# A three-pass attention: the mask carried in 32 contraction rows, the second pass one and a half quads behind, the maxima's parts made on GpSimd

## The chip, the core and the metric

One core of a Trainium2 chip runs the whole program. The metric is device time in microseconds (us). Six layers follow each other in one launch; barriers stand between the stages, so a stage that ends later moves everything behind it.

## The reference, cut to what matters

The layer that is changed is an attention over sets of keys. 4 sequences of 1024 tokens, 16 heads of size 16. The keys are sums over aligned blocks of 4, 8, 16, ... tokens, and a token sees a set only when it lies wholly before or at it; a tail of 1 to 4 tokens is added:

```python
K = _get_slice(k_cum, l_idx, r_idx)          # 511 sets
V = _get_slice(v_cum, l_idx, r_idx)
mask = t[:, None] >= r_idx[None, :]
att_logits = jnp.einsum('bhtd,bhsd->bhts', q, K) * scale
att_logits = jnp.where(mask[None, None], att_logits, -jnp.inf)
att_tail = jnp.sum(q * K_tail, axis=-1) * scale
logits = jnp.concatenate([att_logits, att_tail[..., None]], axis=-1)
att = jax.nn.softmax(logits, axis=-1)
out = jnp.einsum('bhts,bhsd->bhtd', att[..., :-1], V) + att[..., -1:] * V_tail
```

Before it stands a quantised linear layer with a LoRA (`first_ffn`), behind it another one, then a mixture of experts, a linear attention and a second mixture of experts. They are not touched.

## The kernel before

**`first_ffn`** (line 165 on) also makes constants on GpSimd: the identity, a mask `mask_f` of 128 x 256 by 16 affine_select instructions (lines 189 to 201), and flags. VectorE casts the mask to `mask_ts`; TensorE turns it for `mask_st`.

**`attention_front`** (line 507) makes, for each of the 4 sequences, the transposed input, the sums over sets (`larger` on VectorE), the tails (four GpSimd instructions, lines 601 to 604), the projections on TensorE, and three bf16 parts of the queries and keys (`split` on VectorE). The parts go to DRAM. TensorE works in order through a ring of 8 PSUM banks; the product of the sets with the value weights needs the banks that VectorE frees in `products`, which stands behind `sets` and `split` in VectorE's queue.

**`attention_main`** (line 795) works on quads: 4 heads of one sequence, so NQ = 16 quads. `q_hat` and `k_hat` hold one quad: 6 combinations of parts give 96 contraction rows (MROW), rings of 5 buffers. SyncE loads a quad by 12 DMAs of 64 or 128 KB.

- Pass A (`scores_a`) computes tokens by sets, 24 pieces per quad (4 heads, 6 groups of tiles of 128 tokens). Each tile first gets a 128-column matmul with the identity that writes the mask, and then the product is added. VectorE takes the maximum over the sets (`highest`). Three PSUM banks serve pass A, two serve pass B while both run (5 where one runs alone).
- `maxima` on VectorE (step M) joins the tail's logit and splits the negated maxima in three bf16 parts. Step MT turns the parts on TensorE, ScalarE copies them out, and SyncE writes them by 3 DMAs as contraction rows 96 to 98 of `q_hat`; the same rows of `k_hat` hold ones, from a memset at the start.
- Pass B (`scores_b`) computes sets by tokens with 99 rows, 24 pieces per quad: 6 blocks (t = 0 to 5; 512, 256, 512, 512, 512, 256 columns) for 4 heads each. In blocks 0, 1, 4 and 5 a 256-column mask matmul goes first. ScalarE takes the exponential into `prob`.
- `values` multiplies `prob` with the values, two blocks at a time, right after the third block behind has been issued: three bursts per quad.
- O1, O2, O3 (for 8 tiles of each finished sequence, at every 8th step) turn the result, turn the normalised one and project it, all through PSUM bank 7, which MT uses too. VectorE's part of them is `normal` and `update`, GpSimd's is the tail's values (line 938).

The order is one list, STEPS, that every engine walks through. In it, one step of quad i's pass A alternates with one of quad i - 2's pass B:

```python
for i in range(NQ + 2):
    a = [("A", i, h, t) ...] if i < NQ else []
    b = [("B", i - 2, h, t) ...] if i >= 2 else []
```

MT of quad i - 1 stands ahead of step 6. So 48 steps of A run alone, 336 steps run both, 48 steps of B run alone. M stands behind all steps of its quad. SyncE loads quads 1 to 3, the output weights and the router's, and then writes the first maxima.

Of the kernel before, what the change touches and what calls it, by code (L numbers as in the profile page):

```python
# [17 lines left out]
ALU = mybir.AluOpType  # L18
# [112 lines left out]
def first_ffn(nc, s, o, w_dram, b_dram, a_dram, lora_b_dram, x_dram):  # L131
# [35 lines left out]
    with nc.Block(no_gpsimd_drain=True) as block:  # L167
# [13 lines left out]
        def _(pool):  # L181
# [7 lines left out]
            for level in range(7):  # L189
                n, size, at = 64 >> level, 4 << level, P - (P >> level)  # L190
                for half in range(2):

                    v = mask_f[:, half * P + at:half * P + at + n]
                    chain.link(nc.gpsimd.affine_select(out=v, in_=v, compare_op=ALU.is_ge, fill=MASKED,
                                                       base=half * P - size + 1, pattern=[[-size, n]],
                                                       channel_multiplier=1))
            for half in range(2):
                v = mask_f[:, half * P + P - 1:half * P + P]
                nc.gpsimd.affine_select(out=v, in_=v, compare_op=ALU.is_ge, fill=MASKED, base=half * P - 2 * P + 1,
                                        pattern=[[0, 1]], channel_multiplier=1).then_inc(mask_made, 1)  # L200
                pool.wait_ge(mask_made, half + 1)
# [3 lines left out]
            chain.link(nc.gpsimd.affine_select(out=o.row_keep[:, 0:1], in_=o.row_keep[:, 0:1], compare_op=ALU.is_ge,  # L205
                                               fill=0.0, base=P - 2, pattern=[[0, 1]], channel_multiplier=-1))
# [43 lines left out]
        def _(v):  # L250
# [54 lines left out]
            v.wait_ge(mask_made, 2)  # L305
            nc.vector.tensor_copy(o.mask_ts[:].rearrange("p h t -> p (h t)"), mask_f[:])
# [23 lines left out]
        def _(pe):  # L330
# [27 lines left out]
            pe.wait_ge(mask_made, 2)  # L358
# [63 lines left out]
SC = SETS // P  # L422
MASKED = -1e30
# [48 lines left out]
def alloc_attention(nc):  # L472
# [5 lines left out]
    o.mask_ts = sb("mask_ts", [P, 2, P], BF16)  # L478
# [5 lines left out]
    o.k_parts = nc.dram_tensor("k_parts", (BATCH, NPART, C, SETS), BF16, kind="Internal").ap()  # L484
    o.v_tails = nc.dram_tensor("v_tails", (BATCH, P, BT, C), F32, kind="Internal").ap()
# [20 lines left out]

def attention_front(nc, s, o, wqkv_dram):
# [14 lines left out]
    v_tail = sb("v_tail", [P, BT, C])  # L522

# [35 lines left out]
    with nc.Block(no_gpsimd_drain=True) as block:  # L559
        @block.sync  # L560
        def _(sp):
            banks.start(sp)
            sp.dma_start(w[:], wqkv_dram.rearrange("(k p) f -> p k f", p=P)).then_inc(w_in, 16)
            for b in range(BATCH):
# [12 lines left out]
                for n in range(NPART):  # L577
                    sp.wait_ge(k_split, NPART * b + n + 1)
                    sp.dma_start(o.k_parts[b, n].rearrange("(k p) t -> p k t", p=P), k_part[:, z, n]).then_inc(k_out[z], 16)
            for z in range(2):  # L580
                sp.wait_ge(q_out[z], 16 * NPART * BATCH // 2)
                sp.wait_ge(k_out[z], 16 * NPART * BATCH // 2)
            sp.wait_ge(vt_out, 16 * BATCH)
            sp.wait_ge(first_in, 16 * (len(K_PARTS) + len(Q_PARTS)))

        @block.gpsimd
        def _(pool):
            chain = Chain(pool, pool_chain)
            for b in range(BATCH):
# [14 lines left out]
                nc.gpsimd.tensor_tensor(t4[:, :, 3], t4[:, :, 2], x4[:, :, 3], ALU.add).then_inc(tails_made, 1)  # L604

        @block.vector
        def _(v):
# [10 lines left out]
            def larger(of):  # L618

                flat = of.rearrange("p c j i -> p (c j) i")  # L620
                for level in range(1, 7):
                    lo, at, n = P - (2 * P >> level), P - (P >> level), 64 >> level
                    chain.link(nc.vector.tensor_tensor(flat[:, :, at:at + n], flat[:, :, lo:at:2],
                                                       flat[:, :, lo + 1:at:2], ALU.add))
                pairs = of.rearrange("p c (h j) i -> p (c h) j i", j=2)
                nc.vector.tensor_copy(pairs[:, :, 0, P - 1:P], pairs[:, :, 0, P - 2:P - 1])
# [2465 lines left out]
```

## Time and profile before

| | us |
|---|---|
| median of 3 runs | 1725.73 |
| lowest, highest | 1715.12, 1725.94 |
| the profiled execution, its own time | 1731.76 |
| its span from first to last instruction | 1730.0 |
| `attention_front`, last TensorE work to next stage | about 62 to 200 |
| `attention_main` | about 200 to 592 |

| engine | busy us of the span |
|---|---|
| PE (matmul) | 1430.8 (83%) |
| PEld (weight load) | 1072.4 (62%) |
| DVE (VectorE) | 987.9 (57%) |
| ACT (ScalarE) | 690.3 (40%) |
| POOL (GpSimd) | 561.3 (32%) |

The shares are means over stages with different limits; a stage is read from its own stretch. A matmul's duration in the trace holds its latency. What TensorE can do per time shows in the distance between the starts of matmuls that follow each other, called pitch below.

### The profile page before, as it was taken

To read this page: it belongs to the slowest core of one execution; us is meant where nothing else is said; L and a number is where in the kernel's file an instruction comes from. 1 tells how busy PE (TensorE), PEld (TensorE's weight loads), DVE (VectorE), ACT (ScalarE), POOL (GpSimd) and SP (SyncE) were. 2 spreads that over 40 slices of the span, in tenths; PEclk is the share of its full clock that TensorE was granted. 3 is DMA by queue.
4 is the path that set the end of the run, shared out by engine and by line. 5 is a ranking of instruction groups with operands and counts; after the bars stand their busy time and mean duration, and the time that the engine had idled before them with its cause. 6 is when DMAs were issued, how large, how long until landed. Compare 5 with 4: busy or idle time off the path is not lost. (4 is left out here: it accounts for less than half of the span.)

```text
span 1730.0 us, 26233 instructions
## 1 busy us (share of the span) xinstructions
PE 1430.8 (83%) x9328; PEld 1072.4 (62%) x9328; DVE 987.9 (57%) x2872; ACT 690.3 (40%) x1640; POOL 561.3 (32%) x465
## 2 busy tenths in 40 slices
PE   6899889999999678447999999289895459999993
PEld 5566544555555456227889889166663348888893
DVE  8887777787874488884541111256676855521120
ACT  4222147666666377434422222003333425323221
POOL 6522300000000344304436654322211232637644
PEclk9989989999999889658999999599997569999997
DMA  3034563324210023315769996501112325879983
GB/s 108 19 130 136 126 124 61 81 56 83 46 38 2 1 85 110 149 22 137 233 195 276 237 286 132 138 19 49 37 49 100 120 64 187 270 211 257 263 224 41
DMA packets 113483, 211.95 MB, mean 123 GB/s; under 512 B 20069, under 2 KB 79370, under 8 KB 104138
## 3 DMA queue, kind: packets, MB, share of 16 engines
q1 hardware_dynamic: 87338, 178.93, 32.5%
q0 software_dynamic: 26016, 31.34, 11.6%
q8 instruction: 76, 1.25, 0.3%
q14 instruction: 53, 0.43, 0.1%
HBM read 158.71 MB, written 51.12 MB: 121 GB/s over the span
## 5 line engine op out<-in xcount | busy, mean ns | idle before, releaser
L952 DVE TENSOR_REDUCE attnm_top<-psum 128x1 f32<-128x384 f32 (+3 forms) x384 | 212.7, 596 | 60.6 <-PE psum L1037 56.5
L1174 ACT ACTIVATE attnm_prob<-psum 128x512 f32<-128x512 f32 (+1 forms) x384 | 192.1, 530 | 90.2 <-PE psum L1047 83.6
L2553 DVE SCALAR_TENSOR_TENSOR moe1e_h<-moe1e_gate,psum 128x160 f32<-128x160 f32 x160 | 50.1, 320 | 195.2 <-ACT moe1e_gate L2491 167.5
L2553 DVE SCALAR_TENSOR_TENSOR moe2e_h<-moe2e_gate,psum 128x160 f32<-128x160 f32 x160 | 50.2, 320 | 191.9 <-ACT moe2e_gate L2491 162.2
L2356 POOL DMA_INDIRECT out<-moe2e_y,moe_scatter_i x74 | 116.2, 1570 | 117.7 <-DMA out<-moe2e_y,moe_scatter_i 64.0
L2356 POOL DMA_INDIRECT x_sum<-moe1e_y,moe_scatter_i x74 | 116.1, 1569 | 115.6 <-DMA x_sum<-moe1e_y,moe_scatter_i 68.0
L2425 PE MATMUL psum<-moe2e_xgT,moe_w_up 128*128 128x160 f32 x1024 | 150.0, 304 | 1.0 <-issue 1.0
L2425 PE MATMUL psum<-moe1e_xgT,moe_w_up 128*128 128x160 f32 x1024 | 149.6, 303 | 0.9 <-issue 0.9
L2425 PEld LDWEIGHTS psum<-moe2e_xgT,moe_w_up 128*128 128x128 f32 x1024 | 144.5, 193 | 4.2 <-issue 3.2
L2425 PEld LDWEIGHTS psum<-moe1e_xgT,moe_w_up 128*128 128x128 f32 x1024 | 144.3, 193 | 4.0 <-issue 3.0
L1348 POOL DMA_INDIRECT moe_xg<-xn_rows,moe_gather_i x80 | 84.2, 1053 | 156.8 <-DVE moe_gather_i L1537 92.9
L938 POOL TENSOR_TENSOR attnm_tail_v<-attnm_v_tail,attnm_tail_p 128x256 f32<-128x256 f32 x32 | 19.9, 622 | 345.6 <-PE psum L1089 284.7
L1035 PE MATMUL psum<-attn_mask_ts,ident_bf 128*128 128x128 bf16 x512 | 105.4, 226 | 11.8 <-DVE attnm_top L952 7.9
L1037 PE MATMUL psum<-attnm_k_hat,attnm_q_hat 96*128 96x512 bf16 (+3 forms) x384 | 106.3, 305 | 0.0
L1047 PE MATMUL psum<-attnm_q_hat,attnm_k_hat 99*128 99x512 bf16 (+1 forms) x288 | 98.4, 345 | 1.1 <-ACT attnm_prob L1174 0.3
L2491 ACT ACTIVATE moe2e_gate<-psum 128x160 f32<-128x160 f32 x160 | 47.1, 301 | 107.3 <-PE psum L2425 87.7
L2491 ACT ACTIVATE moe1e_gate<-psum 128x160 f32<-128x160 f32 x160 | 47.2, 302 | 104.0 <-PE psum L2425 88.2
L1035 PEld LDWEIGHTS psum<-attn_mask_ts,ident_bf 128*128 128x128 bf16 x512 | 50.5, 100 | 50.0 <-issue 24.5
L1060 PE MATMUL psum<-attnm_prob,attn_v_aug 128*32 128x512 f32 (+1 forms) x768 | 78.7, 527 | 0.0
L1045 PE MATMUL psum<-attn_mask_st,ident_bf 128*128 128x256 bf16 x256 | 70.2, 276 | 5.2 <-DMA attn_q_first<-attnm_mT 5.1
L87 DVE BATCH_NORM_STATS2 x_stats<-x_res 128x6 f32<-128x256 f32 x128 | 44.5, 411 | 36.8 <-DMA x_res<-x_sum 36.2
L2439 PE MATMUL psum<-moe_w_down,moe2e_h 128*128 128x256 f32 x256 | 61.2, 382 | 2.0 <-DMA moe_w_down<-in_expert_down 2.0
(420 smaller groups left out, 3111.3 us busy)
## 6 DMA issues: line engine op xcount, KB each, us to landing
moe_w_up<-in_expert_up SPq DMA_DIRECT2D x64, 1024.0 KB
moe_w_down<-in_expert_down SPq DMA_DIRECT2D x64, 512.0 KB
attnm_q_hat<-q_parts SPq DMA_DIRECT2D x72, 128.0 KB, 4.7
moe_a_up<-in_adapter_up SPq DMA_DIRECT2D x32, 256.0 KB
q_parts<-attnf_q_part SPq DMA_DIRECT2D x12, 512.0 KB, 2.8
attnm_k_hat<-k_parts SPq DMA_DIRECT2D x72, 64.0 KB, 2.3
x_res<-in_x SPq DMA_DIRECT2D x8, 512.0 KB
v_tails<-attnf_v_tail SPq DMA_DIRECT2D x4, 1024.0 KB, 5.3
```

The costliest lines, as they stand in the source:

```text
L952: nc.vector.tensor_reduce(top[:, n // QUADS % 2, tiles[0]:tiles[-1] + 1, hh:hh + 1], s.ps[:, u.bank, 0:len(tiles) * width].rearrange("p (t ...
L1035: nc.tensor.matmul(out[:, width - P:width], s.identb[:], o.mask_ts[:, tile % 2, :], start=(i == 0), stop=False, skip_group_check=True)
L1037: ins = nc.tensor.matmul(out, q_hat[r][0:MROW, h, tile * P:(tile + 1) * P], k_hat[r][0:MROW, h, 0:width], start=False, stop=True, skip_gro ...
L1045: nc.tensor.matmul(s.ps[:, u.bank, at:at + 2 * P], s.identb[:], o.mask_st[:], start=True, stop=False, skip_group_check=True)
L1047: nc.tensor.matmul(s.ps[:, u.bank, at:GROUP], k_hat[r][0:MROW + NPART, h, j * P:(j + 1) * P], q_hat[r][0:MROW + NPART, h, g * GROUP + at:( ...
L1060: ins = nc.tensor.matmul(s.ps[32 * h:32 * h + 32, u.bank, at:GROUP], o.v_aug[:, first:first + 32], prob[:, i % NPROB, at:GROUP], start=(j ...
L1174: nc.scalar.activation(prob[:, i % NPROB, at:GROUP], s.ps[:, u.bank, at:GROUP], ACT.Exp).then_inc(taken[u.bank], 1)
L1348: pool.indirect_dma_start(self.xg[:, q, k, :], None, self.rows, bass.IndirectOffsetOnAxis(ap=self.gather_i[:, at:at + 1], axis=0), bounds_ ...
L2356: nc.gpsimd.indirect_dma_start(total, bass.IndirectOffsetOnAxis(ap=rows, axis=0), y[:, q, k, :], None, bounds_check=TOKENS + SPARE - 1, oo ...
L2425: ins = nc.tensor.matmul(s.ps[:, u.bank, half * CAP:(half + 1) * CAP], lhsT, xgT[:, q, c, k * CAP:(k + 1) * CAP], start=(c == 0), stop=(c ...
L2491: nc.scalar.activation(gate[:, i, :], s.ps[:, u.bank, 0:CAP], ACT.Silu).then_inc(silu, 1)
L2553: nc.vector.scalar_tensor_tensor(out=h[:, HELD[n], i, :], in0=gate[:, i, :], scalar=1.0 if i < INTER // P else SCALE_A, in1=s.ps[:, u.bank ...
```

## The change

- **Layout of the sets.** Sets are ordered in 64s (BLOCK), one for each tile of 128 tokens, instead of 128s for two tiles. Tile k needs columns 0 to 64(k+1), less one for even k: 2300 columns per head instead of 2560.
- **The mask of pass A** goes into contraction rows 96 to 127: `k_hat` carries 0 or -1e30, `q_hat` 1 or 0, so that a tile's own 63 to 65 columns use 128 rows and the columns before them 96. The identity matmuls of pass A go. VectorE's maximum is one instruction per tile: 8 per head instead of 6.
- **The rows** are made on GpSimd in `attention_front`, between the tails of the first and of the second sequence (`make_rows`), written to DRAM, and loaded with each quad by 2 more DMAs: 32 rows for quads 0 to 4, 3 rows later.
- **Order.** LAG = 38: pass B runs 38 steps behind pass A instead of 48. M moves behind the first step of the next quad, MT ahead of step 7, the O steps with the lag. Quad 3, the output weights and the router's are loaded behind the first maxima.
- **GpSimd.** M on VectorE keeps one instruction; GpSimd makes the three parts by 5 chained instructions, the last quad's tail difference, and the ones of `k_hat` by one memset per quad.
- In `first_ffn` 16 affine_select become a memset and 7; the cast to `mask_ts` goes.

```diff
+LAG = NI + NI // 2 + 2
-            b = [("B", i - 2, h, t) for t in range(len(B_BLOCKS)) for h in range(QUAD)] if i >= 2 else []
-                if n == 6 and 1 <= i <= NQ:
+                if n == 7 and 1 <= i <= NQ:
                     yield ("MT", i - 1, None, None)
+                if n == 0 and 1 <= i <= NQ:
+                    yield ("M", i - 1, None, None)
+                if 0 <= NI * i + n - LAG < len(second):
+                    yield second[NI * i + n - LAG]
-            if a:
-                yield ("M", i, None, None)
...
             def scores_a(n, h, t):
-                    nc.tensor.matmul(out[:, width - P:width], s.identb[:], o.mask_ts[:, tile % 2, :], start=(i == 0), stop=False,
-                                     skip_group_check=True)
-                    ins = nc.tensor.matmul(out, q_hat[r][0:MROW, h, tile * P:(tile + 1) * P], k_hat[r][0:MROW, h, 0:width],
+                for tile in A_TILES[t]:
+                    first, own, end = columns(tile, A_TILES[t])
+                    if own > first:
+                        nc.tensor.matmul(s.ps[:, u.bank, first:own], q_hat[r][0:MROW, h, rows], k_hat[r][0:MROW, h, 0:own - first], ...)
+                    ins = nc.tensor.matmul(s.ps[:, u.bank, own:end], q_hat[r][:, h, rows], k_hat[r][:, h, own - first:end - first], ...)
...
+            def make_rows():
+                chain.link(nc.gpsimd.memset(of_set[:], 0.0))
+                for level in range(LEVELS):   # 6 affine_select of 32 to 1 columns
...
+                chain.link(nc.gpsimd.memset(of_token[:], 1.0))   # and 2 affine_select of 128 columns
+                repeat(o.k_first[MROW:P], of_set[MROW:P, :], BLOCK).then_inc(rows_made, 1)
+                repeat(o.q_first[MROW:P], of_token[MROW:P, :], P).then_inc(rows_made, 1)
+                if b == 0:
+                    pool.wait_ge(tails_made, 1)
+                    make_rows()
...
+            def ones(n):
+                pool.wait_ge(full[u.bank], u.after(0))
+                nc.gpsimd.memset(k_hat[n % RQ][MROW:MROW + NPART].rearrange("d h t -> d (h t)"), 1.0).then_inc(ones_made, 1)
+            def maxima(n):
+                chain.link(nc.gpsimd.tensor_scalar(mp[:, :, 0], of, -1.0, None, ALU.mult))
+                chain.link(nc.gpsimd.tensor_tensor(m_res[:], of, mp[:, :, 0], ALU.add))
+                chain.link(nc.gpsimd.tensor_scalar(mp[:, :, 1], m_res[:], -1.0, None, ALU.mult))
+                chain.link(nc.gpsimd.tensor_tensor(m_res[:], m_res[:], mp[:, :, 1], ALU.add))
+                nc.gpsimd.tensor_scalar(mp[:, :, 2], m_res[:], -1.0, None, ALU.mult).then_inc(m_split, 1)
```

`repeat` is one GpSimd tensor_copy from a float32 row of 64 or 128 elements, repeated, to 2048 or 4096 bf16 elements on 32 partitions.

## Rows read from the trace of the kernel before

**Rows 1.** Busy time by stretch: PE, PEld, DVE, ACT, POOL, granted clock, DMA share, GB/s.
```profile
233.30:535.80 302.50, 294.56 (x2428) 166.45 (x2427) 237.16 (x533) 204.18 (x402) 14.26 (x23) 0.99 0.30 61
252.40:272.10 19.70, 19.08 (x164) 9.74 (x162) 14.27 (x30) 14.12 (x28) 0.00 (x0) 1.00 0.30 62
422.70:446.50 23.80, 23.12 (x191) 14.11 (x190) 19.65 (x47) 15.14 (x30) 1.87 (x3) 1.00 0.29 52
535.80:569.30 33.50, 30.64 (x227) 14.20 (x229) 8.13 (x27) 25.38 (x57) 1.87 (x3) 1.00 0.01 2
201.40:233.30 31.90, 21.66 (x142) 11.36 (x140) 27.09 (x59) 1.00 (x1) 15.82 (x41) 0.77 1.01 151
...
76.00:200.00 124.00, 118.04 (x481) 81.13 (x479) 98.48 (x168) 30.73 (x57) 28.34 (x13) 0.93 0.36 120
```

**Rows 2.** Timeline of PE from 440 us: start, duration, engine, line, work.
```profile
440.01 0.22 PE L1035 MATMUL psum<-attn_mask_ts,ident_bf 128*128 128x128 bf16 x1
440.07 0.22 PE L1037 MATMUL psum<-attnm_k_hat,attnm_q_hat 96*128 96x128 bf16 x1
...
440.24 0.27 PE L1045 MATMUL psum<-attn_mask_st,ident_bf 128*128 128x256 bf16 x1
440.35 0.38 PE L1047 MATMUL psum<-attnm_q_hat,attnm_k_hat 99*128 99x512 bf16 x1
440.57 0.60 PE L1081 MATMUL psum<-ident,attnm_oT 128*128 128x128 f32 x4
...
441.77 1.92 PE L1060 MATMUL psum<-attnm_prob,attn_v_aug 128*32 128x512 f32 x16
...
446.31 1.03 PE L1099 MATMUL psum<-attnm_wp,attnm_onT 128*128 128x256 f32 x4
```

**Rows 3.** Timeline of PE in attention_front, a matmul of 8 columns.
```profile
100.57 4.28 PE L742 MATMUL psum<-attn_head_sum,attnf_prod 128*128 128x8 f32 x32
```

**Rows 4.** Timeline of DVE from 200 us.
```profile
214.34 0.24 DVE L963 TENSOR_TENSOR attnm_top<-attnm_top,attn_tail_l 128x32 f32<-128x32 f32 x1
...
215.53 12.31 DVE L952 TENSOR_REDUCE attnm_top<-psum 128x2 f32<-128x256 f32 x24
```

**Rows 5.** Timeline from 272 us: ACT in block 3 of pass B.
```profile
283.28 2.17 ACT L1174 ACTIVATE attnm_prob<-psum 128x512 f32<-128x512 f32 x4
```

**Rows 6.** The same timeline: PE behind M, and the maxima's way to the rows.
```profile
273.76 0.23 PE L1035 MATMUL psum<-attn_mask_ts,ident_bf 128*128 128x128 bf16 x1 [0.59 <-DVE attnm_top L952]
...
276.94 0.61 PE L1070 MATMUL psum<-ident_bf,attnm_m_part 128*12 128x128 bf16 x8
...
277.65 1.00 ACT L1141 COPY attnm_mT<-psum 12x1024 bf16<-12x1024 bf16 x1 [0.21 <-PE psum L1070]
...
278.85 1.83 SPq L905 DMA_DIRECT2D attnm_q_hat<-attnm_mT  x3
```

**Rows 7.** Waits between 235 and 535 us: total, times, longest.
```profile
PE psum L1089 <- ACT attnm_mT L1141: 3.7, 5, 1.0
```

**Rows 8.** Timeline at the start of attention_main: PE's first of pass B.
```profile
232.45 0.40 PE L1045 MATMUL psum<-attn_mask_st,ident_bf 128*128 128x256 bf16 x1 [5.08 <-DMA attn_q_first<-attnm_mT]
```

**Rows 9.** Timelines of attention_front: DVE, POOL and PE.
```profile
74.22 2.12 POOL L604 TENSOR_TENSOR attnf_tailT<-attnf_tailT,attnf_xnT 128x512 f32<-128x512 f32 x1
...
79.74 6.92 DVE L623 TENSOR_TENSOR attnf_setT<-attnf_setT 128x256 f32<-128x256 f32 x6
84.08 2.12 POOL L604 TENSOR_TENSOR attnf_tailT<-attnf_tailT,attnf_xnT 128x512 f32<-128x512 f32 x1
95.36 0.89 PE L696 MATMUL psum<-attnf_w,attnf_setT 128*128 128x256 f32 x3 [2.98 <-DVE attnf_kT L670]
...
110.12 1.66 DVE L623 TENSOR_TENSOR attnf_setT<-attnf_setT 128x256 f32<-128x256 f32 x6
```

**Rows 10.** POOL: the affine_selects at 2 us, and a cast (mean ns).
```profile
2.00 5.05 POOL L194 TENSOR_SCALAR_AFFINE_SELECT ffn_mask_f<-ffn_mask_f 128x64 f32<-128x64 f32 x14
...
L1264 POOL CAST same_b<-same_e 128x128 bf16<-128x128 f32 x1 | 0.3, 292 | 0.1
```

More of the change, by code:

```diff
@@ L188, in _ @@
             chain.link(nc.gpsimd.memset(mask_f[:], 0.0))
[L189 to L201, printed above, removed]
+            chain.link(nc.gpsimd.memset(mask_f[:, BLOCK - 1:P], MASKED))
+            blocks = mask_f[:].rearrange("p (a i) -> p a i", i=BLOCK)
+            for level in range(LEVELS):
+                n, size, at = 32 >> level, 4 << level, BLOCK - (BLOCK >> level)
+                v = blocks[:, 0:4:3, at:at + n]
+                chain.link(nc.gpsimd.affine_select(out=v, in_=v, compare_op=ALU.is_ge, fill=MASKED, base=1 - size,
+                                                   pattern=[[0, 2], [-size, n]], channel_multiplier=1))
+            v = blocks[:, 2:4, BLOCK - 1:BLOCK]
+            nc.gpsimd.affine_select(out=v, in_=v, compare_op=ALU.is_ge, fill=MASKED, base=1 - P, pattern=[[0, 2], [0, 1]],
+                                    channel_multiplier=1).then_inc(mask_made, 1)
+            pool.wait_ge(mask_made, 1)
             chain.link(nc.gpsimd.memset(o.row_keep[:], 1.0))
@@ L819, in attention_main, with columns @@
     A_TILES = [(0, 1), (2, 3), (4,), (5,), (6,), (7,)]
+    def columns(tile, tiles):
+        first = 0 if tile == tiles[0] else BLOCK * (tiles[0] + 1)
+        own = first + BLOCK * tile - tile % 2
+        return first, own, first + BLOCK * (tile + 1) - (tile + 1) % 2
     B_BLOCKS = [(0, 0, 0), (0, 1, 256), (1, 0, 0), (1, 1, 0), (1, 2, 0), (1, 3, 256)]
     NI = QUAD * len(A_TILES)
+    LAG = NI + NI // 2 + 2
     def backs():
@@ L826, in backs @@
         for b in range(BATCH - 1):
-            first = NI * (QUADS * b + QUADS + 2) + 10
+            first = NI * (QUADS * b + QUADS) + LAG + 10
             for k in range(BT):
@@ L924, in _ @@
         def _(pool):
[L925 to L928 removed]
             router.constants(nc, pool)
[L930 to L941 removed]
+            chain = Chain(pool, pool_chain)
@@ L943, in _ @@
+            for kind, n, h, t in STEPS:
+                if kind == "M":
+                    maxima(n)
+                    ones(n)
+                elif kind == "O1":
+                    tail_values(n, h)
+            for k in range(BT):
+                tail_values(LAST, k)
         @block.vector
@@ L948, in highest, with with_tails @@
                 u, tiles = u_a[n, h, t], A_TILES[t]
-                width = (tiles[0] // 2 + 1) * P
                 v.wait_ge(full[u.bank], u.after(0))
                 hh = n % QUADS * QUAD + h
-                nc.vector.tensor_reduce(top[:, n // QUADS % 2, tiles[0]:tiles[-1] + 1, hh:hh + 1],
-                                        s.ps[:, u.bank, 0:len(tiles) * width].rearrange("p (t n) -> p t n", n=width),
-                                        AX_X, ALU.max).then_inc(taken[u.bank], 1)
-            def maxima(n):
+                for tile in tiles:
+                    first, _, end = columns(tile, tiles)
+                    ins = nc.vector.tensor_reduce(top[:, n // QUADS % 2, tile, hh:hh + 1], s.ps[:, u.bank, first:end], AX_X, ALU.max)
+                ins.then_inc(taken[u.bank], 1)
+            def with_tails(n):
                 b, q, z = n // QUADS, n % QUADS, n // QUADS % 2
@@ L1011, in _ @@
                 elif kind == "M":
-                    maxima(n)
+                    with_tails(n)
                 elif kind == "TW":
```

167 lines of the change are left out of this document (101 added, 66 removed).

## The prediction

> **What bounds the kernel.** I read the busy time by stretch first. While both passes run (233.3 to 535.8 us) PE is busy 294.6 of 302.5 us, DVE 237, ACT 204 [rows 1]. A busy PE is not yet a full one, so next the timeline: the pitches say how long TensorE needs. A mask of 128 columns takes 0.058 us, as does a product of 128 columns; (four starts in 0.23); the 256-column mask 0.11, a product of 512 columns 0.22; a burst of values 1.92 for two blocks of 512, three quarters of it for the other pairs [rows 2]. A quad without O steps lasts 19.7 us, one with them 23.8 [rows 1]. Adding the pitches gives 18.2 us for the first: 1568 ns for pass A's mask and products per head, x4 = 6.3; pass B's 1540 ns x4 = 6.2; three bursts with their gaps 5.0; MT 0.7. So PE is the bound, with 1.5 us of stalls per quad. Their places: 0.6 us behind M, where VectorE is away from pass A's banks for 1.19 us (214.34 to 215.53) [rows 4, 6]; and the rest in blocks 2 and 3, where pass B has two banks and follows ScalarE's 0.54 us per 512-column exponential (2.17 / 4 [rows 5]), while PE would need 0.48 for a step (0.26 of pass A, 0.22 of pass B). Outside: before 233 us, pass B waits for the first maxima until 232.45, 5.1 us of it with PE stopped, because they queue behind bulk loads at 151 GB/s [rows 1, 8]. In the front, PE waits once, 2.98 us until 95.36, for VectorE's `products` [rows 9].
>
> **Pass A on PE.** Removed per head: 8 masks x 58 = 464 ns and products of 1104. Added: 7 products of 63, 128, 191, 256, 319, 384 and 447 columns, at 58, 58, 82, 109, 135, 162, 189 (the pitch per column of [rows 2], 58 as least) = 793, and 8 of 63 to 65 columns. No row shows a bf16 matmul so short. Its bounds: 29 ns, half of the 128-column pitch, and 58, all of it. The nearest row in kind is the float32 one of 8 columns, 4.28 / 32 = 134 ns each [rows 3], no shorter than the 110 of float32 transposes of 128 columns (0.44 for four [rows 2]): weights and issue then set the pitch. I take 58: 464. Sum 1257, a saving of 311 ns per head, 1.24 us per quad. With 29 it were 2.3 us.
>
> **Quads without O.** 19.7 - 1.24 - 0.6 (M leaves VectorE but for one instruction of 0.24 [rows 4]; its chain on GpSimd, 5 x about 0.35 us by the affine_select pitch of 5.05 / 14 [rows 10], has 7 steps, about 5 us, until MT). Blocks 2 and 3 stay on ScalarE's pace, so their part of the PE gain is lost, and MT with ScalarE's 1.00 us copy [rows 6] moves into them: +0.15 net, as TensorE has 0.7 us of its own work there. 18.0 us.
>
> **Quads with O.** PE is full there, ScalarE and VectorE are not [rows 1]: 23.8 - 1.24. The shared bank 7 changes: the old stall (O2 behind MT: 3.7 us in 5 [rows 7]) goes, but MT now stands directly behind an O3, so TensorE waits until VectorE has added that result, about 1.0 us, and O1 follows one step later. Net +0.4: 23.0 us.
>
> **VectorE** has 24 maxima in 12.31 us [rows 4]. Two more instructions per head at some 0.07 us and 260 fewer columns at 1.04 ns: 11.8. It isn't the bound.
>
> **The maxima's way.** MT to the first of three DMAs takes 1.91 us, and their issue 1.83 [rows 6]: 3.7, and a landing of 1 to 2. Before, 18 steps stood between MT and the quad's pass B; now 7, with one burst: MT 0.8, 7 pieces of A and B 3.4, burst 2.0, so 6.2 us. It just fits: no cost taken. The memset of ones is done long before.
>
> **The start.** Ahead of the first maxima stand two loads of 1.54 MB instead of three of 1.15 with weights: 3.07 MB at 151 GB/s [rows 1] from 202 us on is 222.4. The copy of the maxima is done before, at about 218.5: 213.7 for the first quad's maxima, some 3 us to MT, 1.7 for MT and copy. Pass B starts at 222.5 instead of 232.45 [rows 8], with 38 steps of pass A done.
>
> **The sum for attention_main.** Both passes then run for 346 steps. O steps stand in 176 of them (7.33 quads), 170 are without (7.08): 7.33 x 23.0 + 7.08 x 18.0 = 296.0, until 518.5. Pass B alone took 33.5 us for 48 steps with 3.2 O tiles [rows 1], each about 1.5 (0.44 to turn, half of that to turn back, 0.86 to project [rows 2]): 0.6 per step. Now 38 steps and 2 tiles: 25.7, until 544.2 instead of 569.3: **-25.1 us**. What follows is the same.
>
> **The front pays.** At 79.74, six additions of VectorE take 6.92 us beside GpSimd's tails, and the same six 1.66 at 110.12 with GpSimd idle [rows 9]: an addition with two SBUF inputs waits for the GpSimd instruction in progress, one per instruction. (The Trainium skill, SBUF — State Buffer, Who interferes with whom, says that such an instruction contends with a GpSimd one that reads SBUF, and that the shared port is an exclusive lock; the trace agrees, 6.92 against 1.66 us.) So `sets` of sequence 0 ends when GpSimd ends, at 86.2 + 0.9. `make_rows` goes in ahead of the second tails: from 76.4 (74.22 + 2.12 [rows 9]), some 3.5 us of small instructions (8 affine_select x 0.36, three memsets), and casts of 2048 and 4096 elements. The cast of 128 takes 292 ns [rows 10], nearly all of it fixed or 1 ns per element; at 1.05 they cost 2.3 and 4.5 (bounds 0.9 and 2: 5.5 or 12.3 together). GpSimd reaches the tails at 87, and ends at 94 instead of 86.2. VectorE has nine instructions left to slip one by one between six of GpSimd. `split` and `products` move by the same, and TensorE's wait at 92.4, which had no slack, becomes 10.5 us: **+7.5 us** (6 to 13). Behind it TensorE is busy almost throughout (118.0 of 124 us from 76 to 200 [rows 1], and 3.4 of the 6 are this wait and one of 0.45), so little is given back. In `first_ffn` GpSimd's constants are 3 us shorter and the first rstd 0.6 earlier: -0.5. `larger` keeps its element count, one instruction more: nothing.
>
> **Total.** -25.1 + 7.5 - 0.5 = -18.1: the profiled 1731.8 becomes 1713.7. It lies 6 us above the median of the runs; on that median 1725.7 - 18.1 = **1707.6**.
>
> **Rivals.** (1) Short matmuls cost 29 ns: 9 x 29 x 4 = 1.04 us per quad more, whole in quads with O (7.6), 0.4 us where ScalarE bounds (2.9): 1697. (The Trainium skill, TensorE: Matmul & The Clock Gate, Back-to-back issue gap, gives about 25 ns as the issue floor for 1 to 64 columns; by it, an estimate of 1696. Against it stands only the float32 row; no bf16 row decides.) (2) The front's cost is hidden because the casts are short or VectorE gets past GpSimd: 1700. Against it: four of six additions took GpSimd's time. (3) The PE gain is swallowed by the two- and three-bank rings while both passes run: only M's 0.6 per quad and the lag count, 346 x 0.903 - 8 = 304: 1716. For it speak blocks 2 and 3, against it the quads with O. (4) The other side: the maxima land too late for 7 steps. TensorE then stops in each of 15 quads in front of pass B, and pass A behind it in the same queue. The first landing stopped PE for 5.1 us behind bulk loads [rows 8]. The loads of a quad now start with pass B's and have about 17 steps until the next maxima, so it should not recur. A landing 4.8 us after the last issue, 2.3 over the 2.5 that fit, costs 15 x 2.3 = 35: 1742. Slower than before it is from 3.7 us on (18.1 / 15 over), slower by 1% from 4.9.
>
> **Chances.** Forecast 0.42; (1) 0.20; (2) 0.10; (3) 0.18; (4) 0.10. About 1% is what a measurement of this kernel can tell from no change: below 1708.5 is faster, above 1743 slower. The forecast straddles the first bound, three in five below. So faster 0.42 x 0.6 + 0.20 + 0.10 = 0.55, slower 0.05, same 0.40. The range reaches from rival 1 with short casts, 1694, to rival 3 with long ones, 1722.
>
> **What would show it.** Pass B's first matmul at 222.5 + 7; quads of 18.0 and 23.0 us; own-column matmuls at a pitch of 58; a PE wait for VectorE of 10 us near 92; no PE wait for the maxima's DMA except the first. The forecast fails if that last wait recurs, if a short matmul's pitch is far from 58, or if the front's wait stays at 3.

## The result, and the profile after

| | before | after |
|---|---|---|
| median of the runs, us | 1724.34 | 1759.53 (1753.63 to 1765.25) |
| ratio, 95% interval | | 1.0215 (1.0175 to 1.0254) |
| span of the profiled execution | 1730.0 | 1763.5 |
| first to last exponential of pass B | 233.3 to 569.1 | 233.6 to 614.5 |
| end of `attention_main` | 590.4 | 635.9 |

The changed kernel is slower by 2.1%, where 1707.6 us and a gain were forecast. By the end of `attention_main` the profiles lie 45.5 us apart: 7.3 us are there when the front ends, the rest arises in `attention_main`. (The whole profiles end only 33.5 us apart. The profile of before shows 393.6 us in its first mixture of experts and 392.2 in its second; after and every experiment show 385 to 386 and 384 to 389, with the same code there. One of them is experiment 10, the kernel before with one edit in `attention_main`, so this is scatter between executions and none of the change's.)

Part 1 and the clock's row of part 2 of the page of the kernel after (its columns are the engines; the second row holds 40 equal slices of the span). GpSimd's busy time is up by 49 us to 610.3; TensorE's busy time is unchanged, though a tenth of pass A's columns and all its masks are gone. In its clock the slices from 309 to 397 us and from 485 to 573 us show 8, 7, 8 and 8 tenths; before had 9 or more there:

```profile
PE 1430.1 (81%) x9264; PEld 1073.0 (61%) x9264; DVE 968.1 (55%) x2931; ACT 687.5 (39%) x1640; POOL 610.3 (35%) x565
...
PEclk9989879879988989955999999789998559999997
```

The busy time by stretch of the kernel after; the columns are those of [rows 1]. The stretches are: a quad without O steps, two with them, and the start up to pass B's first matmul.

```profile
262.00:280.40 18.40, 17.52 (x157) 8.70 (x156) 12.42 (x35) 13.70 (x28) 3.16 (x6) 1.00 0.24 53
317.30:347.20 29.90, 25.84 (x197) 15.71 (x199) 18.48 (x53) 15.54 (x32) 5.03 (x9) 0.83 0.42 90
347.20:377.50 30.30, 25.44 (x190) 15.32 (x186) 18.41 (x53) 15.02 (x31) 5.02 (x9) 0.83 0.26 45
207.80:232.80 25.00, 15.89 (x108) 8.57 (x108) 19.29 (x54) 1.00 (x1) 11.02 (x42) 0.50 0.99 148
```

The quad without O steps is near what was forecast, 18.4 us (18.0). The quads with O steps last 30 us; 23.8 was before's [rows 1], 23.0 the forecast. Two things are different in them: PE is idle for 4 to 5 us, and the mean granted clock is 0.83 instead of 1.00 (0.82 to 0.94 over the eight). Eight quads have O steps; they last 27.6 to 30.3 us and sum to 230.3, where 8 x 23.0 is 184. That is 46 of the 55 us by which the stretch with both passes (351.4 us for 346 steps) exceeds the forecast of 296.0; the other 9 are a quad at the start with a lower clock (21.6), 0.4 us in each quad without O steps, and the count: O steps touch 8 whole quads, not 7.33.

What happens in one such quad stands in the timeline of the kernel after from 346 us. The columns are start, duration, engine, line, work; what ended an idle time is in brackets.

```profile
347.18 0.18 DVE L1053 TENSOR_TENSOR attnm_top<-attnm_top,attn_tail_l 128x32 f32<-128x32 f32 x1
347.27 0.17 DVE L1067 TENSOR_TENSOR attnm_den<-psum,attnm_tail_p 128x16 f32<-128x16 f32 x1
347.51 0.29 POOL L1000 TENSOR_SCALAR attnm_m_part<-attnm_top 128x32 bf16<-128x32 f32 x1 [21.66 <-issue]
...
348.93 0.29 POOL L1004 TENSOR_SCALAR attnm_m_part<-attnm_m_res 128x32 bf16<-128x32 f32 x1
349.27 1.80 POOL L989 MEMSET attnm_k_hat<- 3x2048 bf16 x1
351.16 1.32 POOL L1019 TENSOR_TENSOR attnm_tail_v<-attnm_v_tail,attnm_tail_p 128x256 f32<-128x256 f32 x2
351.88 0.42 DVE L1069 TENSOR_TENSOR attnm_tail_v<-psum,attnm_tail_v 128x256 f32<-128x256 f32 x1 [4.44 <-POOL attnm_tail_v L1019]
...
352.84 2.07 DVE L1044 TENSOR_REDUCE attnm_top<-psum 128x1 f32<-128x191 f32 x5
353.58 0.50 PE L1115 MATMUL psum<-attnm_k_hat,attnm_q_hat 96*128 96x384 bf16 x1 [4.25 <-DVE attnm_top L1044]
```

Read it from the bottom. TensorE stands for 4.25 us until VectorE has emptied a bank of pass A. VectorE hadn't begun on it, because ahead in its queue stands `normal` (L1069), which waits 4.44 us for the tail's values from GpSimd. GpSimd had stood idle for 21.66 us until the maximum of L1053 was there, and then worked through what stands in its queue at that step: five instructions for the parts (1.76 us with their gaps), the memset of the ones (1.80), and only then the tail's values of the same step (0.62 each). O1 stands 38 + 10 = 48 steps behind its quad, which is step 0 of a quad again: the very step at which M stands. The quad's next matmuls run at the lower of TensorE's two levels, 1.2 GHz: the 384-column product takes 0.50 us here and 0.33 in a quad that doesn't stop, and the granted clock is 0.50 (columns as in [rows 1]):

```profile
353.40:357.00 3.60, 3.42 (x15) 2.25 (x16) 2.53 (x7) 1.72 (x4) 0.62 (x1) 0.50 0.02 5
```

The waits of the kernel after from 200 to 620 us (total, times, longest) count it. VectorE's nine are one per quad with O steps and one where pass B runs alone. Of TensorE's nine, eight are those quads' stops, 3.45 to 4.67 us and 32.4 us together; the ninth is 1.76 us at 229 us, at the start, which experiment 1 has too. The stop in pass B alone is in another row, 3.73 us at 590 us. Before has no wait for `tail_v`:

```profile
DVE attnm_tail_v L1069 <- POOL attnm_tail_v L1019: 40.6, 9, 4.9
PE psum L1115 <- DVE attnm_top L1044: 34.2, 9, 4.7
```

In the kernel before, GpSimd had nothing to do in this stage but the tail's values. It was always one tile ahead and waited itself: this is its timeline from 333 us.

```profile
341.42 0.62 POOL L938 TENSOR_TENSOR attnm_tail_v<-attnm_v_tail,attnm_tail_p 128x256 f32<-128x256 f32 x1 [8.65 <-PE psum L1089]
```

### The profile page after: what moved, and what is told of

It reads as the page before. It is cut to its first block and busy times, and to the rows that moved or that the text cites. A ratio compares the mean times of both kernels' runs of the same rounds, so it can differ in the third digit from the quotient of the medians.

```text
span 1763.5 us, 26326 instructions
## 1 busy us (share of the span) xinstructions
PE 1430.1 (81%) x9264; PEld 1073.0 (61%) x9264; DVE 968.1 (55%) x2931; ACT 687.5 (39%) x1640; POOL 610.3 (35%) x565
## 5 line engine op out<-in xcount | busy, mean ns | idle before, releaser
L1044 DVE TENSOR_REDUCE attnm_top<-psum 128x1 f32<-128x63 f32 (+7 forms) x512 | 200.1, 449 | 72.1 <-PE psum L1117 69.6
L1427 POOL DMA_INDIRECT moe_xg<-xn_rows,moe_gather_i x80 | 84.2, 1053 | 158.1 <-DVE moe_gather_i L1616 93.0
L1115 PE MATMUL psum<-attnm_k_hat,attnm_q_hat 96*128 96x63 bf16 (+6 forms) x336 | 91.6, 296 | 26.5 <-DVE attnm_top L1044 26.5
L1127 PE MATMUL psum<-attnm_q_hat,attnm_k_hat 99*128 99x512 bf16 (+1 forms) x288 | 104.9, 367 | 2.9 <-ACT attnm_prob L1253 2.5
L1000 POOL TENSOR_SCALAR attnm_m_part<-attnm_top 128x32 bf16<-128x32 f32 x16 | 4.6, 288 | 281.4 <-issue 262.4
L1117 PE MATMUL psum<-attnm_k_hat,attnm_q_hat 128*128 128x63 bf16 (+1 forms) x384 | 68.4, 205 | 2.5 <-DMA attnm_q_hat<-q_parts 2.5
L1115 PEld LDWEIGHTS psum<-attnm_k_hat,attnm_q_hat 96*128 96x128 bf16 x336 | 34.9, 105 | 51.0 <-DVE attnm_top L1044 28.6
L2518 PE MATMUL psum<-moe_w_down,moe1e_h 128*128 128x256 f32 x256 | 61.1, 382 | 1.6 <-DMA moe_w_down<-in_expert_down 1.6
```

Of the source, the lines that this page charges most:

```text
L1044: ins = nc.vector.tensor_reduce(top[:, n // QUADS % 2, tile, hh:hh + 1], s.ps[:, u.bank, first:end], AX_X, ALU.max)
L1115: nc.tensor.matmul(s.ps[:, u.bank, first:own], q_hat[r][0:MROW, h, rows], k_hat[r][0:MROW, h, 0:own - first], start=True, stop=True, skip_ ...
L1127: nc.tensor.matmul(s.ps[:, u.bank, at:GROUP], k_hat[r][0:MROW + NPART, h, j * P:(j + 1) * P], q_hat[r][0:MROW + NPART, h, g * GROUP + at:( ...
L1427: pool.indirect_dma_start(self.xg[:, q, k, :], None, self.rows, bass.IndirectOffsetOnAxis(ap=self.gather_i[:, at:at + 1], axis=0), bounds_ ...
L2518: ins = nc.tensor.matmul(s.ps[:, u.bank, 0:C], h[:, HELD[n], i, 0:P], down_weight(k, i), start=(i == 0), stop=(i == PAIRS - 1))
```

## Experiments

The theory ("the queue"): the tail's values stand behind the parts and the ones in GpSimd's queue; `normal` on VectorE waits for them, pass A's maxima wait behind `normal`, and TensorE waits for the banks. Rivals: bank 7, shared by MT and the O steps, holds TensorE; or GpSimd's instructions slow VectorE's wherever they overlap, so that order doesn't matter. The first four kernels ran on one chip beside each other and before (1720.72 us). Experiments 5 to 8 ran on a second chip (before 1719.69), 9 and 10 on a third (1721.05), 11 on a fourth (1719.71), so across them the ratios are compared.

**The order of GpSimd's queue.** The tail's values of tile k + 2 are issued at O2 of tile k, the first two of a sequence as soon as their factors are known:

```diff
-                elif kind == "O1":
-                    tail_values(n, h)
-            for k in range(BT):
+                elif kind == "TW":
+                    tail_values(n, 0)
+                    tail_values(n, 1)
+                elif kind == "O2" and h + 2 < BT:
+                    tail_values(n, h + 2)
+            for k in range(2, BT):
```

> The changed kernel with one edit: GpSimd issues the tail's values of tile k right where tile k-2 is turned (step O2), and tiles 0 and 1 at TW, instead of at the step O1 of tile k. No instruction is added, taken away or moved on another engine. Theory (the queue): in each quad with O steps one tail value stands in GpSimd's queue behind the five instructions of the maxima's parts and the memset of ones, all issued at the quad's first step, and VectorE, which has reached the same tile, waits for it 4.4 us with pass A's banks held; the changed kernel shows this wait 9 times, 40.6 us, plus the half clock after each stop. Then the wait goes, quads with three O tiles take 22 to 24 us instead of 28 to 30, and the time falls by 45 to 60 us, to about 1705. Rival 1 (bank 7): MT directly behind O3 and the turns behind MT are what lengthens these quads; then this edit takes away at most the 5 us of PE waits that are not behind the tail values, and the time stays above 1745. Rival 2 (shared port): VectorE is slowed because GpSimd now works beside it; the edit leaves all of that work, the time stays at 1755 to 1765.

Measured: 1710.78 us, ratio 0.9950 (0.9934 to 0.9967). The wait for the tail's values is gone from the waits. The eight quads with O steps last 178.0 us together instead of 230.3, at full clock:

```profile
317.80:340.90 23.10, 22.29 (x198) 13.44 (x199) 18.41 (x52) 15.06 (x32) 5.03 (x9) 1.00 0.56 121
```

`attention_main` ends 56.5 us sooner than after (579.4 and 635.9); the medians lie 48.7 us apart. Nothing was taken from GpSimd: the same instructions in another order. So the rivals fall. Of the 52 us that the eight quads give back, 32 are TensorE's stops (4.1 us each). The other 20 are what TensorE lost at the lower clock behind the stops: the same matmuls keep it busy for 191 us of these quads in after and for 170 here, and in after the clock is 0.50 for 3 to 10 us behind every stop.

**The ones later.** Only the memset of the ones leaves its place, to the next step of pass A:

```diff
-                    ones(n)
+                    waiting = n
...
+                if waiting is not None and kind in ("A", "MT"):
+                    ones(waiting)
+                    waiting = None
```

> The changed kernel with one edit: GpSimd's memset of ones is issued behind the next step's pass A, so behind the tail's value of the quad's first step, not ahead of it. The parts stay ahead. Theory (the queue): the wait of VectorE shrinks by the memset's 1.8 to 1.9 us, from 4.4 to 2.6 us, in 8 quads: 15 us, and up to 10 more if the shorter stop keeps TensorE's clock at its upper level: 1735 to 1745. Rival 1 (bank 7) and rival 2 (shared port): the memset's place doesn't matter, 1755 to 1765.

Measured: 1737.06 us, ratio 1.0077 (1.0051 to 1.0102). The same two waits:

```profile
DVE attnm_tail_v L1073 <- POOL attnm_tail_v L1019: 23.9, 9, 3.0
PE psum L1119 <- DVE attnm_top L1048: 19.3, 9, 2.8
```

40.6 - 23.9 = 16.7 us, over 9 that is 1.86 us, the memset and its gap. The time falls with what stands ahead of the tail's values, as the theory had it (1735 to 1745); the rest are the parts. The eight quads last 201.6 us.

**The rows later.** `make_rows` behind the tails of the third sequence instead of the first, on the kernel after:

```diff
-                if b == 0:
-                    pool.wait_ge(tails_made, 1)
+                if b == 2:
+                    pool.wait_ge(tails_made, 3)
                     make_rows()
```

> The changed kernel with one edit: the mask's rows are made behind the tails of the third sequence instead of the first, and written out there. Theory (the front's step of the prediction): VectorE's additions of sequence 0 then wait only for GpSimd's tails, TensorE's stop near 93 us is 3 us again instead of 8.2 to 9, the front ends 6 to 7 us earlier, the time falls by as much: 1752. Rival: TensorE's work behind the stop has slack somewhere later, or the same waits come at the third sequence: no change.

Measured: 1754.79 us, ratio 1.0207 (1.0190 to 1.0224). In its profile TensorE's wait in the front is 3.14 us, and the front ends at 196.1 us instead of 204.7; its intervals and after's overlap, so the time alone would not show it.

**Both**, the new order and the late rows:

> The edits of e1_pool_order and e3_rows_late together. If both theories hold and the stages follow each other, the gains add: about 7 us below e1_pool_order, near 1698, 1.5% below the kernel before. By rival 1 or 2 only the front's 7 us come: 1752.

Measured: 1703.38 us, ratio 0.9895 (0.9877 to 0.9913), so 7.4 us off the first experiment on the same chip: that is what the place of the rows costs. TensorE's wait in the front, of after and of this kernel:

```profile
101.33 6.68 PE L742 MATMUL psum<-attnf_w,attnf_setT 128*128 128x256 f32 x16 [8.16 <-DVE attnf_kT L716]
```

```profile
96.14 5.38 PE L742 MATMUL psum<-attnf_w,attnf_setT 128*128 128x256 f32 x16 [2.96 <-DVE attnf_kT L716]
```

This kernel is the base of those that follow. The experiments ask what its remaining parts are worth, since it beats before by 1% where the forecast without the front's cost says 1.5%.

**The lag.** `LAG = 2 * NI`, 48 steps as before instead of 38:

> e4_both with pass B two whole quads behind pass A (LAG 48 instead of 38), so 17 steps between MT and the quad's pass B instead of 7. Theory: the shorter lag is worth what pass B alone takes for 10 steps, about 6 us, less what pass A's ten steps cost ahead of pass B, part of which stands in PE's wait of 2.5 us for the first maxima: 3 to 6 us slower than e4_both, attention_main's part with both passes 336 steps long. Rival: the wait for the first maxima (about 25 us after the stage begins) takes up the whole of it, and the lag is worth nothing: within 1.5 us of e4_both. Second rival: O2 and O3 now stand around MT at bank 7, as in the kernel before: then the quads with O steps are 0.5 to 1 us longer each (23.5 instead of 22.6), and it is 8 to 12 us slower.

Measured: 1694.29 us, ratio 0.9853 (0.9822 to 0.9883), 0.4% faster than with 38. All three expectations miss. The shorter lag costs: `attention_main` takes 366.5 us instead of 371.0. (The fronts differ by 2.7 us more, 130.7 and 133.3, with the same code; over all kernels with late or no rows they scatter from 130.3 to 133.6.) Pass B can't start before the first maxima have landed, some 25 us after the stage begins (first exponentials 26.0 and 24.9 us behind its start). With a lag of 48 pass A uses that time for ten more steps, and these ten then don't stand beside pass B; that gives back more than the end takes, where from pass A's last product to the last exponential it is 34.3 us instead of 27.2. And the second maxima, 17 steps ahead instead of 7, are waited for 0.8 us instead of 2.5; the quad with that wait takes 19.2 us instead of 22.2. MT between O2 and O3 cost nothing: the four quads that share a sequence's 8 O tiles last 84.2 us, 84.5 in the base.

**The parts on VectorE.** M as in the kernel before, five instructions on VectorE; GpSimd keeps the ones and the tail's values:

```diff
-                    maxima(n)
...
+                chain.link(nc.vector.tensor_scalar(mp[:, :, 0], top[:, z, :, heads], -1.0, None, ALU.mult))
...
+                nc.vector.tensor_tensor(mp[:, :, 2], m_res[:], mp[:, :, 1], ALU.subtract).then_inc(m_split, 1)
```

> e4_both with the three parts of the maxima and the tail difference made by VectorE again, in five chained instructions at step M; GpSimd keeps the ones and the tail values. The prediction took 0.6 us per quad as the price of this stay away from pass A's banks, so by it this is 15 x 0.6 = 9 us slower than e4_both. Rival: VectorE works 12.4 us of a quad's 18.4, and a delay of 1 us at the start of a quad is made good behind the next burst of values, so nothing is lost: within 2 us of e4_both, quads without O steps at 18.4 us.

Measured: 1699.95 us, ratio 0.9882 (0.9844 to 0.9919), not to be told from the base. Quads without O steps last 18.4 us as before this edit; those with O steps 0.3 to 0.8 us longer (23.1, 23.1 and 21.8 instead of 22.7, 22.4 and 21.0). So moving the parts to GpSimd, the move that brought the loss, had at most some 5 us to win (0.3 to 0.8 in eight quads). That they don't show in the time has a reason at the start: this kernel doesn't wait for the second maxima at all, and that quad takes 18.4 us, not 22.2. Whether VectorE's parts do that, or the scatter of this wait (0 to 3.4 us in the eight kernels with the lag of 38), isn't shown.

**The price of the masks.** A 128-column identity matmul per tile back in front of pass A's products, 32 x 58 ns = 1.86 us per quad; the products overwrite it:

```diff
+                for tile in A_TILES[t]:
+                    nc.tensor.matmul(s.ps[:, u.bank, 0:P], s.identb[:], o.mask_st[:, 0:P], start=True, stop=True, ...)
                 for tile in A_TILES[t]:
```

> e4_both with an identity matmul of 128 columns per tile put back ahead of pass A's products (32 per quad, overwritten by the products, so the result is the same): the price of the mask matmuls that the change took away, 32 x 0.058 = 1.86 us of TensorE per quad. If TensorE is the bound in all quads: 16 x 1.86 = 30 us slower than e4_both. If in quads without O steps the banks' rings set the pace (their TensorE time by pitches is 14.9 of 18.4 us, and would be 16.7), only the 8 quads with O steps and pass A alone pay it: 15 us slower, and quads without O steps stay within 0.4 us of 18.4.

Measured: 1709.03 us, ratio 0.9925 (0.9896 to 0.9953), 0.3% or 5 us over the base, where 30 or 15 were expected. A quad without O steps takes 0.4 us more (18.8), one with them 0.7 to 0.9 more:

```profile
253.80:272.50 18.70, 18.49 (x190) 10.47 (x188) 12.59 (x34) 13.89 (x28) 3.17 (x6) 1.00 0.37 68
310.30:334.20 23.90, 23.25 (x227) 15.13 (x225) 18.60 (x52) 15.32 (x31) 5.04 (x9) 1.00 0.51 109
```

Of 1.86 us of TensorE's time only a quarter to a half stays in such a quad. TensorE is busy in the first stretch by the records (18.49 of 18.70), and yet in the base it was nearly as busy (17.51 of 18.40) with 1.86 us less to do: a busy PE isn't a full one. The start pays 2.4 us back: with the added matmuls the quad at 233 us takes 19.8 us at a clock of 1.00, in the base 22.2 at 0.92, and the wait for the second maxima in it is 1.0 us instead of 2.5.

**A third bank for pass B.** The sums over values, two per quad and never both open, share bank 5, and bank 6 joins pass B's ring:

```diff
-            u_b[q, h, t] = banks.use(3 + nb % 2 if nb < NI * NQ - LAG else nb % 5)
+            u_b[q, h, t] = banks.use((3, 4, 6)[nb % 3] if nb < NI * NQ - LAG else nb % 5)
-                u_o[q, t // 2] = banks.use(5 + t // 2)
+                u_o[q, t // 2] = banks.use(5)
```

> e4_both with three PSUM banks instead of two for pass B while both passes run; the third is one of the two that held the sums over values, which now share one. If the two-bank ring sets the pace of quads without O steps (ScalarE works 13.7 us of 18.4 and stands still for 1.8 us in each of the three bursts of values), a third bank gives it work to do in a burst: 16 to 17 us per such quad, 7 of them, and 0.5 us off each quad with O steps: 12 to 20 us faster than e4_both. If pass A's three banks, or TensorE's own order, set the pace: within 3 us of e4_both.

Measured: 1685.75 us, ratio 0.9802 (0.9769 to 0.9835), 0.9% better than the base and as expected. Its quads without O steps last 16.3 us:

```profile
252.40:268.70 16.30, 16.30 (x160) 8.49 (x156) 12.21 (x34) 12.92 (x28) 3.16 (x6) 1.00 0.28 63
```

The two-bank ring was the bound of such a quad in the mended kernel. ScalarE had two results to work on in a burst of values and then stood still. The longest such time of a quad is 1.84 us in the base and 1.43 with the third bank (the other two bursts 0.86 and 0.86, then 0.71 and 0.86, not the 1.8 in each that the expectation took); over the quad ScalarE is idle for 4.7 and then 3.4 us. The timeline of the base, from 265 us:

```profile
265.07 1.68 ACT L1256 ACTIVATE attnm_prob<-psum 128x256 f32<-128x256 f32 x4 [1.84 <-PE psum L1130]
```

**Third bank and lag 48 together:**

> e8_third_bank with pass B two whole quads behind pass A, as in e5_lag_48. By e5 against e4 (attention_main 366.5 instead of 371.0 us in the profiles) it is 3 to 7 us faster than e8_third_bank, ratio 0.976 to 0.978: what the shorter lag takes off the end it adds at the start, where pass A stands still until the first maxima have landed. Rival: with quads of 16.3 us instead of 18.4 the ten steps of pass B alone at the end (8 us in e5) outweigh the start: 0 to 4 us slower than e8.

Measured: 1683.22 us, ratio 0.9781 (0.9738 to 0.9824), 0.2% under the eighth kernel and inside both intervals; in the profiles `attention_main` is 3.0 us longer (355.2 and 352.2), so this run doesn't decide between expectation and rival. One quad lasts 23.9 us; TensorE stops there once, for the second quad's maxima, as the waits from 200 to 620 us show:

```profile
PE psum L1128 <- DMA attnm_q_hat<-attnm_mT: 4.5, 1, 4.5
```

**The third bank in the kernel before,** nothing else of the change:

> The kernel before with the third PSUM bank for pass B alone, nothing else of the change. If TensorE was its bound, as the prediction read it (18.2 us of pitches in a quad of 19.7), at most 1.5 us of each quad without O steps can go, 8 of them, and nothing of those with: up to 12 us faster than before, quads of 18.2 us. If the two-bank ring was its bound, it gains what e4 gained, 2.1 us per quad without O steps and 1 to 0.4 per quad with them: 16 to 20 us faster than before, and then the change (mask rows, order, GpSimd) is worth the rest of e8's or e9's distance.

Measured: 1712.29 us, ratio 0.9953 (0.9934 to 0.9972). Its quads without O steps last 18.8 us instead of 19.7, those with them 23.7 instead of 23.8. That is 8.8 us, well short of what the ring gives the mended kernel: before was near TensorE's own limit, as the prediction read it (18.8 us against 18.2 of pitches), and only in part bound by the ring. So neither cure shows its worth alone: with two banks the masks are worth 0.4 us of a quad without O steps (experiment 7), and with the masks and 260 more columns per head the third bank is worth 0.9, where without them it gives 2.1. Once both have three banks, the rest of the change takes 2.5 us off such a quad (18.8 and 16.3).

**Quad 4 loaded later,** behind the second maxima instead of ahead of them, on the ninth kernel:

```diff
+                if i == 2:
+                    load(RQ - 1)
...
-                if i + RQ - 2 < NQ:
+                if 2 <= i and i + RQ - 2 < NQ:
```

> e9_bank_lag_48 with quad 4 loaded behind the second maxima instead of ahead of them (it is read only at 266 us; the load of 1.54 MB stood in flight when the second maxima were written at 237.65 us, and TensorE waited 4.5 us for them). If the bulk load ahead of them was the reason, TensorE's wait for the second maxima's DMA goes, the quad falls from 23.9 to about 19, and the kernel is 3 to 5 us faster than e9_bank_lag_48: ratio 0.975 to 0.976. If quad 3, the output weights and the router's, issued from 220 us on, are what stands ahead, the wait stays above 2 us and the time within 2 us of e9.

Measured: 1674.45 us, ratio 0.9741 (0.9714 to 0.9768). The wait is gone from the waits, as it should be if quad 4's load stood ahead of the second maxima; with one profile of each kernel, and a wait that scatters (0.8 us in experiment 5 with the load in the same place), that is likely and not proven. The quad lasts 16.2 us, and at full clock:

```profile
241.40:257.60 16.20, 16.18 (x157) 8.61 (x156) 12.22 (x34) 12.71 (x28) 3.17 (x6) 1.00 0.86 159
```

`attention_main` takes 348.3 us instead of 355.2, more than the 3 to 5 us expected; the intervals of the two ratios still overlap. This is the fastest of all kernels here, 2.6% faster than before and 4.6% than after (0.9741 / 1.0215). It keeps the mask rows, the columns and the GpSimd parts of the change; the lag of 38, the place of the rows and the order of GpSimd's queue are gone.

| kernel | median us | ratio to before |
|---|---|---|
| after | 1759.53 | 1.0215 |
| 1, GpSimd's order | 1710.78 | 0.9950 |
| 2, the ones later | 1737.06 | 1.0077 |
| 3, the rows late | 1754.79 | 1.0207 |
| 4, 1 and 3 together | 1703.38 | 0.9895 |
| 5, 4 with lag 48 | 1694.29 | 0.9853 |
| 6, 4 with the parts on VectorE | 1699.95 | 0.9882 |
| 7, 4 with mask matmuls | 1709.03 | 0.9925 |
| 8, 4 with the third bank | 1685.75 | 0.9802 |
| 9, 8 with lag 48 | 1683.22 | 0.9781 |
| 10, before with the third bank | 1712.29 | 0.9953 |
| 11, 9 with the late load | 1674.45 | 0.9741 |

## Why the prediction was wrong, step by step

**The step that failed** stands in "Quads without O": M's "chain on GpSimd ... has 7 steps, about 5 us, until MT". Its size was right (5 x 0.35 us forecast, 1.76 measured) and so was its slack: MT never waited long for it. But the step asked only who waits for the chain. It never named what is queued behind it on GpSimd, and in the same way "the memset of ones is done long before" gave the memset no price. Behind both stood the tail's values of the same step, behind those VectorE's `normal`, behind that pass A's banks. "Quads with O: 23.0" took over the price of before plus 0.4 for bank 7, and so left this out. It cost 32 us of stops and 20 us through the clock in eight quads. Two choices of the change meet in it, the work moved to GpSimd and the lag of 38, by which O1 falls on M's own step; the kernel after with a lag of 48, where the nearest O1 stands two steps behind M, wasn't run. None of the rivals had it. Rival 4 had the shape, a stop in every quad by which the sign turns, but in another queue.

**The other terms**, in the prediction's order:

- *Short matmuls at 58 ns: mis-sized.* 63 to 65 columns with weights of their own follow each other at 0.03 to 0.04 us (half of them within 0.033 in experiment 4). The timeline of the kernel after:

```profile
402.72 0.20 PE L1117 MATMUL psum<-attnm_k_hat,attnm_q_hat 128*128 128x63 bf16 x1
402.76 0.20 PE L1115 MATMUL psum<-attnm_k_hat,attnm_q_hat 96*128 96x63 bf16 x1
402.79 0.20 PE L1117 MATMUL psum<-attnm_k_hat,attnm_q_hat 128*128 128x65 bf16 x1
```

  The lower bound of 29 ns was nearly right, the float32 row [rows 3] the wrong neighbour. (The Trainium skill, TensorE: Matmul & The Clock Gate, Back-to-back issue gap, gives about 25 ns as the issue floor; here the trace is close, 30 to 40 ns.) By rival 1 it was to bring 1697. In the mended kernel it didn't, because the ring held the quads as well as TensorE: by the seventh experiment a quarter to a half of TensorE's time counts.
- *Quads without O, 18.0 us: near in sum (18.4), and that by luck, for its terms were off.* The 0.6 us for M's leaving was nothing (experiment 6), and of the masks' 1.86 us only 0.4 shows (experiment 7). Where the rest of 19.7 - 18.4 comes from is open; the fewer columns, 260 per head, and the new order may each have a part.
- *Quads with O, 23.0: right once mended.* With GpSimd's order changed the eight last 22.2 us on average, those with all three O tiles 22.7. The wait of MT behind an O3 took 0.6 us at most, where 1.0 was forecast.
- *The maxima's way: right but once.* The maxima of the second quad came late: 1.9 us in the kernel after, 0 to 3.4 in the others with the lag of 38, 0.8 and 4.5 with 48 (experiments 5 and 9). That is rival 4 in one quad out of 15. "The loads of a quad now start with pass B's" was true of all later ones; at the start quad 4's load stood between the first and the second maxima, and with it moved, in experiment 11, the wait is gone.
- *The start, 9.9 us sooner: 6.1.* 25.0 us from the stage's begin to pass B's first matmul instead of 31.05. The writes of the maxima were issued 18.2 us behind the stage's start, 1 us later than computed, but pass B could start only 3.9 us later than computed; TensorE stood still for 3.3 us of them ([rows 8] has the row that it answers to):

```profile
232.79 0.39 PE L1125 MATMUL psum<-attn_mask_st,ident_bf 128*128 128x256 bf16 x1 [3.27 <-DMA attn_q_first<-attnm_mT]
```

  148 GB/s for 25.0 us are 3.7 MB, 0.6 more than the two loads counted. From 228.0 us on, ahead of the landing, SyncE had issued quad 3's load, 0.8 MB of it by 232.3; whether holding it back would bring the maxima sooner wasn't tried.
- *The lag of 38 as a gain: wrong,* by experiment 5. The working let pass B start at 222.5 + 7 with pass A's 38 steps just done, and counted the ten steps saved at the end. It left out that pass A, 48 steps of it, would have filled the same wait.
- *Pass B alone, 25.7 us:* 30.35, one of the nine stops; 25.6 in experiment 1.
- *The front, +7.5: right in size.* Its end comes 7.3 us later (204.7 and 197.5), and 7.4 us lie between experiments 1 and 4. The terms are smaller: TensorE's wait was 8.2 us where 10.5 was forecast, 5.2 longer than before; behind it the clock was 0.50 for 10.2 us instead of 3.4, and the front as a whole takes 139.8 us instead of 133.6. The rest is its start, 1.1 us later than before. The -0.5 for `first_ffn` doesn't show; over the kernels the front's start scatters from 63.4 to 65.6 us. The casts took 1.89 and 3.60 us (2.3 and 4.5 forecast), together the lower bound of 5.5.
- *Rival 3's 304 us:* [rows 1] give 0.900 us per step (302.5 / 336), not 0.903, so it is 303.5.

Taken together, the mended kernel needs 349.7 us from the start of `attention_main` to the last exponential, and before 367.7: 18.0 us gained where 25.1 were forecast. The missing 7 are the start (3.8), the quad with the wait for the second maxima, at a clock of 0.92 (3.9), and the 0.4 us of each quad without O steps, less what the quads with O steps did better.

## What to carry to other kernels

When work moves to an engine that seemed idle, list what that engine already does at the step where the new work lands, and who waits for it: a queue is served in order, and an engine that is 32% busy may be the one that hands over one small thing at a time. Let work that depends on nothing new (here the tail's values) be issued ahead of work that waits for the newest result. And price TensorE's savings only after the rings are counted: in the mended kernel one more bank gave 2.1 us per quad without O steps, and 1.86 us less of matmuls had given 0.4.

## What the hardware did that was not expected

- A stop of about 4 us cost TensorE more than itself: behind the one at 349.3 us the granted clock was 0.50 (353.4 to 357.0 us), and the eight quads lost about 20 us that way beside 32 us of stops. In experiment 2 the stops were 1.6 to 2.8 us. Behind the three of 1.59 us the clock stayed at 1.00 (the quad at 318.7 us has one); behind four of 2.4 to 2.8 us it fell to 0.50 (the quad from 343.3 us has a mean of 0.93), behind another of 2.4 us it didn't.
- Not every VectorE instruction pays for GpSimd's long ones. In the front of after an addition of four columns with both inputs in SBUF took 2.07 us beside a GpSimd addition of 2.12 us (the same line's took 0.17 us at 105.39, with GpSimd idle). In `attention_main` a maximum over 447 columns of PSUM took 0.61 us on average in the 14 cases that lay wholly within a 1.80 us memset of GpSimd, and 0.62 in the 50 others (experiment 4). A memset reads nothing, but beside GpSimd's multiplications of the tail's values, which do, it was the same: the 28 maxima that lay mostly within one took, on average of their width, at most 0.01 us longer than the others.

```profile
88.95 2.12 POOL L640 TENSOR_TENSOR attnf_tailT<-attnf_tailT,attnf_xnT 128x512 f32<-128x512 f32 x1
89.01 2.07 DVE L670 TENSOR_TENSOR attnf_setT<-attnf_setT 128x4 f32<-128x4 f32 x1
```
- A GpSimd instruction on 32 columns takes 0.25 to 0.29 us and starts, when chained, 0.34 to 0.38 us after its forerunner. A memset of 3 partitions x 2048 bf16 takes 1.80 us and the casts of 32 x 2048 and 32 x 4096 elements 1.89 and 3.60, each about 0.9 ns per element of one partition, and a memset of 128 partitions x 512 float32 takes 0.53 us, 1.0 ns: what counts in these rows is the length of a row, and 3 partitions are no cheaper than 128.
